# Graph layers on one core: VectorE reads a body's 18 tile numbers in one load, the sum banks go round in another order, and the mixer's rows are fetched between the two table stores

## The reference, cut to what matters

```python
for l in range(4):                                    # L0_gnn, one "loop" each below
    h = einsum('ni,rio->rno', X, W[l])                # the tables: one row per relation and node
    msg = h[etype, src] * inv_deg[:, None]
    agg = segment_sum(msg, dst)                       # 100,000 messages into 6,250 nodes
    out = agg + X @ root[l] + bias[l]
    X = elu(layer_norm(out) * gamma[l] + beta[l]) + X
...
qkv = x @ Wqkv.T                                      # L0_mix, on the same nodes
q, k = elu(q) + 1, elu(k) + 1
kv, ksum = k^T v, sum(k)                              # Keys0
x1 = layer_norm(q kv / (q ksum + eps) + x)            # Attend
y = layer_norm(gelu(x1 @ W1.T + b1) @ W2.T + b2 + x1) # Feed
...
agg = segment_sum(all_h[src, rel], dst)               # L1_gnn, 8 relations: loop gnn1
```

## Time and profile before

| | |
|---|---|
| median of 3 runs | 8250.26 us (8244.22 to 8263.54) |
| profiled execution, its own time | 8245.88 us |
| its span, first to last instruction | 8244.1 us |
| mean granted clock of TensorE | 0.823 |
| PE / PEld busy | 5874.8 us (71%) / 3559.1 us (43%) |
| DVE busy | 4269.0 us (52%) |
| ACT busy | 2931.9 us (36%) |
| POOL busy | 4208.5 us (51%) |

### The profile page before, as it was taken

The page is one execution under the profiler, slowest core; times in us unless marked ns, Lnnn a source line. Parts: engine busy times, 40 slices in busy tenths (PEclk is TensorE's granted clock), DMA queues, the critical chain, the costliest instruction groups (busy, mean ns, idle before and its releaser), DMA issues. The chain is left out here.

```text
span 8244.1 us, 110504 instructions
## 1 busy us (share of the span) xinstructions
PE 5874.8 (71%) x17886; PEld 3559.1 (43%) x17886; DVE 4269.0 (52%) x14582; ACT 2931.9 (36%) x8048; POOL 4208.5 (51%) x4288
## 2 busy tenths in 40 slices
PE   0487777767777776777768888788498777763398
PEld 0244444444444444554443333355344444443265
DVE  7215555546666665666656666522434666652412
ACT  0133333333444445666653333222022444431132
POOL 0016666656666656777667777600002777753211
PEclk9998888888888888889985556589599888877699
DMA  1444333334444434444443333300044333330000
GB/s 56 145 132 118 112 116 114 113 115 121 124 124 123 123 117 134 135 135 135 132 151 105 104 105 105 99 0 0 19 142 132 105 105 105 105 87 1 13 14 18
DMA packets 478956, 811.01 MB, mean 98 GB/s; under 512 B 88600, under 2 KB 343148, under 8 KB 478657
## 3 DMA queue, kind: packets, MB, share of 16 engines
q0 software_dynamic: 200480, 548.02, 23.2%
q1 hardware_dynamic: 278430, 262.51, 9.9%
HBM read 614.04 MB, written 196.16 MB: 98 GB/s over the span
## 5 line engine op out<-in xcount | busy, mean ns | idle before, releaser
L530 POOL DMA_INDIRECT gnn_msg<-tables,gnn_row_ring x4165 | 3985.8, 957 | 2183.9 <-issue 1585.2
L579 PE MATMUL bank<-gnn_msg,gnn_hot 128*128 128x256 f32 x8330 | 3143.3, 494 | 781.0 <-DVE sums L559 506.8
L559 DVE TENSOR_TENSOR sums<-sums,bank 128x256 f32 x4165 | 1746.0, 419 | 2060.0 <-PE bank L579 1360.7
L579 PEld LDWEIGHTS bank<-gnn_msg,gnn_hot 128*128 128x128 f32 x8330 | 1748.2, 237 | 2130.3 <-DVE sums L559 1424.8
L133 POOL TENSOR_TENSOR ve<-mv,eps 128x7 f32<-128x7 f32 x35 | 7.1, 204 | 1348.6 <-DVE mv L127 1200.3
L520 ACT ACTIVATE gnn_hot<-gnn_away,gnn_meta_ring 128x128 f32<-128x128 f32 x1568 | 645.8, 482 | 47.3 <-ACT gnn_meta_ring L511 0.8
L684 PE MATMUL bank<-gnn_w,residual 128*128 128x512 f32 x1176 | 620.1, 610 | 33.7 <-DVE sums L652 33.7
L508 ACT ACTIVATE gnn_away<-iota,gnn_meta_ring 128x128 f32<-128x128 f32 x1960 | 625.5, 391 | 24.0 <-ACT gnn_meta_ring L498 0.2
L539 DVE TENSOR_SCALAR gnn_hot<-iota,gnn_meta_ring 128x128 f32<-128x128 f32 x1764 | 629.1, 357 | 0.5 <-ACT gnn_meta_ring L498 0.5
L497 ACT COPY gnn_row_ring<-row 128x9 int32 (+1 forms) x490 | 94.9, 194 | 1070.3 <-PE bank L579 1058.5
L1760 PE MATMUL bank<-tables_w,sums 128*128 128x512 f32 x784 | 340.1, 596 | 6.4 <-ACTq L117 6.4
(11 more groups left out here) (390 smaller groups left out, 6866.1 us busy)
## 6 DMA issues: line engine op xcount, KB each, us to landing
tables<-residual SPq DMA_DIRECT2D x294, 256.0 KB
gnn_msg<-tables,gnn_row_ring POOLq DMA_INDIRECT x4165, 2.8
tables<-sums SPq DMA_DIRECT2D x98, 512.0 KB, 2.9
tables<-gnn_msg SPq DMA_DIRECT2D x98, 256.0 KB, 2.1
residual<-first_norm_columns SPq DMA_DIRECT2D x98, 128.0 KB, 2.4
first_norm<-state SPq DMA_DIRECT2D x1, 6272.0 KB, 21.4
first_rows<-residual SPq DMA_DIRECT2D x1, 6272.0 KB, 39.2
residual<-first_norm SPq DMA_DIRECT2D x49, 128.0 KB, 3.1
```

The costliest lines, as they stand in the source:

```text
L530: self.nc.gpsimd.indirect_dma_start(out=self.msg[:, s0 + u, :], out_offset=None, in_=table, in_offset=bass.IndirectOffsetOnAxis(ap=self.ro ...
L559: self.nc.vector.tensor_tensor(at, at, self.sums(s), ALU.add).then_inc(self.added, 1)
L579: self.nc.tensor.matmul(self.sums(s), self.hot[:, s, :], self.msg[:, s, :], start=True, stop=True).then_inc(self.summed, 1)
```

## The change

Four edits. (1) A row with 18 numbers for each body (the 17 tiles and the tile to finish) takes the place of the flat row, and VectorE loads all 18 at the body's start. (2) The banks of the 17 steps are a written list. (3) `sync` is split into `load` and `store`; the load for body i + 1 stands between the two table stores of body i. (4) Some hooks move to other steps: TensorE's mixer products, and in Attend two VectorE operations change places.

```diff
-SUM_SLOTS = 4
+SUM_BANKS = (4, 5, 6, 7, 4, 5, 6, 7, 4, 5, 6, 4, 5, 6, 4, 5, 6)
...
-def load_tiles(eng, c, first, n):
-
-    regs = c.regs[str(eng.engine)][:n]
-    eng.reg_load(regs, c.tile_row[0:1, ds(first, n)])
+def body_tiles(eng, c, i):
+
+    regs = c.regs[str(eng.engine)]
+    eng.reg_load(regs, c.body_row[0:1, ds(i * (SLOTS + 1), SLOTS + 1)])
     return [eng.snap(r, min_val=0, max_val=NT - 1) for r in regs]
...
-                sp.dma_start(c.tile_row[:], c.tl_d.rearrange("(a n) -> a n", a=1)).then_inc(s_tr, 16)
+                sp.dma_start(c.body_row[:].rearrange("p (i n) -> p i n", n=SLOTS + 1)[:, :, 0:SLOTS],
+                             c.tl_d[0:(NT + 1) * SLOTS].rearrange("(a i n) -> a i n", a=1, n=SLOTS)).then_inc(s_tr, 16)
...
+                ends_of = c.body_row[:].rearrange("p (i n) -> p i n", n=SLOTS + 1)[:, :, SLOTS]
+                then(v.tensor_copy(ends_of[:, 0:1], key[0:1, 0:1]))
+                then(v.tensor_copy(ends_of[:, 1:NT + 1], key[0:1, :]))
...
     def sums(self, s):
-        return self.c.bank[4 + s % SUM_SLOTS][:, 0:D]
+        return self.c.bank[SUM_BANKS[s]][:, 0:D]
...
-            tiles = load_tiles(dve, self.c, i * SLOTS + s0, w)
-            for u, t in enumerate(tiles):
+            for u in range(w):
                 s = s0 + u
+                t = tiles[s]
...
-            back = s - SUM_SLOTS + 1 if s >= SUM_SLOTS else max(k for k in range(SLOTS) if k % SUM_SLOTS == s) + 1 - SLOTS
-            pe.wait_ge(self.added, n * SLOTS + (SLOTS + back))
+            before = max(k for k in range(s - SLOTS, s) if SUM_BANKS[k] == SUM_BANKS[s])
+            pe.wait_ge(self.added, n * SLOTS + (SLOTS + before + 1))
...
 # Keys0.tensor and Attend.tensor
-            if s == 5 and first:
+            if s == 3 and first:
...
 # Attend.vector: L961 to step 6, L964 to step 9
-            if s == 9 and first:
+            if s == 6 and first:
                 dve.wait_ge(self.s_act, i * 2 + 3)
                 v.scalar_tensor_tensor(self.et, self.et, 1.0, self.rt, ALU.min, ALU.add).then_inc(self.s_q, 1)
-            if s == 6 and second:
+            if s == 9 and second:
                 dve.wait_ge(self.s_hat, i + 1)
                 v.tensor_tensor(self.u, self.u, self.vec[:, 0, :], ALU.mult).then_inc(self.s_gam, 1)
...
 # Feed.tensor: steps 3, 6, 10 become 2, 5, 9
...
-                    work.sync(sp, 0, True, False)
-                    with sp.Fori(1, NT) as i:
-                        work.sync(sp, i, True, True)
-                        post.sync(sp, i + l * NT, ranked_tile(sp, c, i - 1), c.tabs[(l + 1) % 2])
-                    work.sync(sp, NT, False, True)
-                    post.sync(sp, (l + 1) * NT, ranked_tile(sp, c, NT - 1), c.tabs[(l + 1) % 2])
+                    work.load(sp, 0)
+                    work.store(sp, 0, True, False)
+                    work.load(sp, 1)
+                    with sp.Fori(1, NT - 1) as i:
+                        t = ranked_tile(sp, c, i - 1)
+                        work.store(sp, i, True, True)
+                        post.sync(sp, i + l * NT, t, c.tabs[(l + 1) % 2], 0)
+                        work.load(sp, i + 1)
+                        post.sync(sp, i + l * NT, t, c.tabs[(l + 1) % 2], 1)
+                    for i in (NT - 1, NT):
+                        t = ranked_tile(sp, c, i - 1)
+                        work.store(sp, i, i < NT, True)
+                        for j in range(2):
+                            post.sync(sp, i + l * NT, t, c.tabs[(l + 1) % 2], j)
...
-                        t = ranked_tile(dve, c, i - 1)
-                        edges.vector(dve, i, n, both(post.vector(dve, n, t, work.cols), work.vector(dve, i, True, True)))
+                        tiles = body_tiles(dve, c, i)
+                        edges.vector(dve, tiles, n, both(post.vector(dve, n, tiles[SLOTS], work.cols),
+                                                         work.vector(dve, i, True, True)))
...
-        c.tile_row = sb("tile_row", [1, SB * P], I32)
+        c.body_row = sb("body_row", [1, (NT + 1) * (SLOTS + 1)], I32)
```

More of the change, by code:

```diff
@@ L548, in begin_vector, with vector @@
             self.one_hot(0, u)
-    def vector(self, dve, i, n, after, last=False):
+    def vector(self, dve, tiles, n, after, last=False):
         for h, (s0, w) in enumerate(HALVES):
-            tiles = load_tiles(dve, self.c, i * SLOTS + s0, w)
-            for u, t in enumerate(tiles):
+            for u in range(w):
                 s = s0 + u
+                t = tiles[s]
                 dve.wait_ge(self.summed, n * SLOTS + (SLOTS + s + 1))
@@ L701, in way_out, with sync @@
         self.nc.scalar.copy(self.outs[:, j, :], self.c.bank[3 - 2 * j][:]).then_inc(self.s_out, 1)
-    def sync(self, sp, n, t, table):
-        for j in range(2):
-            sp.wait_ge(self.s_out, n * 2 + (j + 1))
-            sp.dma_start(table.rearrange("(r n) d -> n r d", n=NP)[ds(t * P, P), 2 * j:2 * j + 2, :],
-                         self.outs[:, j, :].rearrange("p (r d) -> p r d", d=D)).then_inc(self.s_store[j], 16)
+    def sync(self, sp, n, t, table, j):
+        sp.wait_ge(self.s_out, n * 2 + (j + 1))
+        sp.dma_start(table.rearrange("(r n) d -> n r d", n=NP)[ds(t * P, P), 2 * j:2 * j + 2, :],
+                     self.outs[:, j, :].rearrange("p (r d) -> p r d", d=D)).then_inc(self.s_store[j], 16)
 def tile_columns(c, i):
@@ L731, in begin_sync, with load, store @@
         sp.dma_start(self.wt, self.c.wt_d[:, :, D:3 * D]).then_inc(self.s_in, 16)
-    def sync(self, sp, i, first, second):
-        if first:
-            sp.wait_ge(self.s_mm, i + 1)
-            sp.dma_start(self.xt.rearrange("p h r -> p (h r)"), tile_columns(self.c, i)).then_inc(self.s_xt, 16)
+    def load(self, sp, i):
+        sp.wait_ge(self.s_mm, i + 1)
+        sp.dma_start(self.xt.rearrange("p h r -> p (h r)"), tile_columns(self.c, i)).then_inc(self.s_xt, 16)
+    def store(self, sp, i, first, second):
+        return None
     def end_sync(self, sp):
@@ L896, in begin_sync, with load, store @@
         sp.sem_inc(self.s_dma, 16)
-    def sync(self, sp, i, first, second):
+    def load(self, sp, i):
         c = self.c
-        if first:
-            sp.wait_ge(self.s_u, i + 1)
-            sp.dma_start(self.xt.rearrange("p h r -> p (h r)"), tile_columns(c, i)).then_inc(self.s_xt, 16)
-            sp.dma_start(self.x, c.xn_d[ds(i * P, P), :]).then_inc(self.s_x, 16)
+        sp.wait_ge(self.s_u, i + 1)
+        sp.dma_start(self.xt.rearrange("p h r -> p (h r)"), tile_columns(c, i)).then_inc(self.s_xt, 16)
+        sp.dma_start(self.x, c.xn_d[ds(i * P, P), :]).then_inc(self.s_x, 16)
+    def store(self, sp, i, first, second):
+        c = self.c
         if second:
@@ L1008, in begin_sync, with load, store @@
         sp.sem_inc(self.s_put, 16)
-    def sync(self, sp, i, first, second):
+    def load(self, sp, i):
+        sp.wait_ge(self.s_u, i + 1)
+        sp.dma_start(self.x, self.c.rows_d[ds(i * P, P), :]).then_inc(self.s_dma, 16)
+    def store(self, sp, i, first, second):
         c = self.c
-        if first:
-            sp.wait_ge(self.s_u, i + 1)
-            sp.dma_start(self.x, c.rows_d[ds(i * P, P), :]).then_inc(self.s_dma, 16)
         if second:
@@ L1041, in after @@
         def after(s):
-            if s == 3 and first:
+            if s == 2 and first:
                 pe.wait_ge(self.s_dma, i * 16 + 16)
@@ L1046, in after @@
                 self.turn(pe, self.x, c.bank[0])
-            if s == 6 and first:
+            if s == 5 and first:
                 pe.wait_ge(self.s_xt, i + 1)
                 self.by_columns(self.w1)
-            if s == 10 and first:
+            if s == 9 and first:
                 pe.wait_ge(self.s_act, i * 2 + 3)
@@ L1371, in _ @@
                     gate(dve, c)
-                    edges.vector(dve, 0, l * NT, work.vector(dve, 0, True, False))
+                    edges.vector(dve, body_tiles(dve, c, 0), l * NT, work.vector(dve, 0, True, False))
                     dve.wait_ge(s_vec, l * 48 + 96)
@@ L1382, in _ @@
                 gate(dve, c)
-                edges.vector(dve, 0, LASTL * NT, nothing)
+                edges.vector(dve, body_tiles(dve, c, 0), LASTL * NT, nothing)
                 dve.wait_ge(s_vec, LASTL * 48 + 96)
@@ L1386, in _ @@
                     n = i + LASTL * NT
[L1387 to L1390 removed]
+                    tiles = body_tiles(dve, c, i)
+                    edges.vector(dve, tiles, n, post.vector(dve, n, tiles[SLOTS], 1, last=True))
+                tiles = body_tiles(dve, c, NT - 1)
+                edges.vector(dve, tiles, DEPTH * NT - 1, post.vector(dve, DEPTH * NT - 1, tiles[SLOTS], 1, last=True), last=True)
                 t = ranked_tile(dve, c, NT - 1)
@@ L2491, in program @@
                    (("pe", nc.tensor), ("act", nc.scalar), ("dve", nc.vector), ("pool", nc.gpsimd), ("sp", nc.sync))}
-        c.regs = {str(e.engine): [e.alloc_register(f"tile{u}") for u in range(HALF)] for e in (nc.vector,)}
```

(1 more changed line is left out.)

10 lines of the change are left out of this document (3 added, 7 removed).

## The result

The changed kernel takes 8053.94 us (median of 4 runs, 8048.98 to 8055.62), the kernel before 8256.88 us on the same chip (4 runs, 8244.22 to 8263.54): a ratio of 0.9753, 95% interval 0.9738 to 0.9767. The forecast was 8054.

A forecast was written before the change was run, and what follows sets the result against it. GpSimd's issue bounds loop 3 and gnn1, an alternating VectorE and TensorE chain loops 0 to 2. Terms of -33, -149, -10, 0 and 1 us of preparation, hidden or not, sum to -192 from 8245.9: 8054 us, range 7980 to 8185.

The forecast's parts named there:

- One load at the seam: Between bodies, add 16 to add 0: mean 4.5 us against 3.8 now, so 0.7 us longer.
- The load model: VectorE's register loads: 0.08 us fixed, 0.22 per number alone, 0.265 per four together; 18 numbers take 1.58 or 4.05 us.
- the first rival: The 18-number load is never short: seams of 6.08 us in loops 0 to 2, total 8284 us, slower; 9%.
- No load in the middle: Before add 9 in a body: the idle time of the second register load goes, 1.38 us on average.
- Banks at nothing: New bank order of the 17 steps: costs or gains nothing in loops 0 to 2; GpSimd hides waits elsewhere.
- The early fetch: Mixer rows fetched between the table stores, some 3.2 us earlier: gives 0.1 us a body at most in Feed.
- Mixer steps: TensorE's mixer products at earlier steps (5 to 3; Feed 3, 6, 10 to 2, 5, 9): fill seam idle.
- Loop 0, -33: Keys0's loop: -1.38 + 0.7 = -0.68 us a body over 48 bodies, -33 us.
- Attend's swap, L937 at 8.2, chain of 9.6: Loop 1: L937 starts 8.2 us after add 0, then 9.6 to add 16; body 22.3 against 25.4 us, -149 us.
- The third rival: GpSimd becomes the bound in loop 1: +0.4 us a body, 8075 us, inside the forecast's range; no chance given.
- The rule on register loads: Rule against the forecast: about 200 ns a register even for bulk, so 18 numbers take 3.6 us and gathering saves nothing.
- The fourth rival: More comes free: Feed's idle reaches the chain, TensorE's clock is granted more; 1 us a body in loops 0 and 2, 7960 us; 12%.

The follow-up runs named there:

- both experiments on the address: Changed kernel with rows of 20 numbers, every load starting at a multiple of 16 bytes, or none: 7932.8 us and 8287.3 us.
- the load alone: Kernel before with the single load of 18 numbers a body and nothing else of the change: 8138.9 us, ratio 0.9860.
- rows of 20: Changed kernel with 20 numbers per body in the row, 18 used, every load starting at a multiple of 16 bytes: 7932.8 us, ratio 0.9609.
- the fetch behind: Changed kernel with the mixer's next rows fetched behind the second table store again: 8024.7 us, ratio 0.9720 against the kernel before.

## Why the prediction was right, and where it wasn't

The total was right to the microsecond, which is luck: loops 0 and 1 gained 64 us more than forecast, loop 2 lost 50 us against its forecast, and the stretches between and the last two loops lost some 15 us that had no term.

1. *One load at the seam, mean +0.7.* Right: 4.45, 4.49 and 4.44 us in loops 0 to 2, against 3.84, 3.90 and 3.70 (+0.6 to +0.7). The load model read from four rows held for 18 numbers, 1.57 and 4.05 (in the loops with stores the long ones take a median of 4.6, where 4.72 was forecast), and both experiments on the address confirmed it, with the first rival's 8284 as 8287.
2. *No load in the middle, -1.38.* Right at its place (-1.43 to -1.54 between adds 8 and 9). Of it Feed passes on less than the 0.8 that I took: with the load alone, Feed's adds 9 to 16 took 7.22 us against 6.45, and adds 0 to 8 11.28 against 11.01, so only 0.39 of 1.43 reached the end, less than the seam's 0.77. That is the first wrong step: Feed loses 18 us from the load itself.
3. *Banks at nothing.* Right, within 8 us.
4. *The early fetch, 0.1 us at most in Feed.* Wrong in sign: it costs 21 us in loop 2 and 29 in the kernel, although the wait it was to remove (3.40 to 0.45 us) did go. What it sets off in loop 2 is open (below).
5. *Mixer steps "fill the idle at the seam", cost nothing.* Wrong, the dearest miss. They cost 42 us in loop 0 and 19 in loop 2. In the earlier trace rows I looked at who waits for whom, and not at how long the same matmul takes where it stands; L791's 275/422 was to be seen in the trace of before. That is the mistake for loop 0. The 19 us of loop 2 are not the clock's: with the steps back it is as it was (0.68 against 0.67 from add 0 to add 9, 1.00 in both from there to add 16), and what changes is the wait at L879.
6. *Loop 0, -33.* The two load terms as measured make -0.83 us a body (-40 us), and adds 9 to 16 got 0.27 shorter, which had no term. But that is what two large effects left: the load alone gives 105 us, 2.1 us a body and not 0.68, because without the middle load the second half came at the high level in 30 bodies of 42 instead of 3 (L795 median 276, L791 422) and took 9.09 us instead of 10.34; the rest of the change, almost all of it step 5 of this list, took 44 back.
7. *Attend's swap, L937 at 8.2, chain of 9.6.* The mechanism is right and the size too small. L944 starts at 8.76, and the chain behind it takes 8.67 in the body shown and 8.52 on average. The 9.6 was right for the kernel before (mean 9.67), where much of Post's product L678 ran at the low level:

```profile
L678 PE MATMUL bank<-gnn_w,residual x192: 379/634/635, 1879.5 to 3082.0; 128*128 128x256 f32 x192
```

```profile
L682 PE MATMUL bank<-gnn_w,residual x192: 379/379/483, 1815.9 to 2840.2; 128*128 128x256 f32 x192
```

   These are loop 1 before and after: a median of 634 ns, now 379; 135 of 192 records were at the low level, now none. It is the swap that does it: none are with the swap alone, 138 with it undone, and the granted clock from add 9 to add 16 is 0.77 before, 0.78 with the swap undone, 0.94 changed and 1.00 with the swap alone. TensorE without its gap of four microseconds is granted the high level for what follows. So the fall went on until GpSimd stopped it. The third rival (GpSimd becomes the bound in loop 1) came true, at a lower level than it was priced.
8. *The rule on register loads* (the Trainium skill, "Runtime: NRT & Kernel Launch", "Instruction fetch mechanics", 200 ns a register even for bulk): long loads agree, 4.04/18 = 0.22 us; short ones are 1.57/18 = 0.09, and rows of 20 make every load short. That page of the Trainium skill speaks of registers loaded from HBM; here the numbers lie in SBUF.

The fourth rival (TensorE waits less and is granted its clock more often) named the mechanism and gave it to the wrong loops at 12%: the granted clock between first and last add rose from 0.842 to 0.848 in loop 0 and from 0.847 to 0.866 in loop 1, and fell from 0.893 to 0.824 in loop 2; the mean of the kernel fell from 0.823 to 0.809.

**What stays open.** In loop 2 the two ways to undo the earlier work are each worth 20 us and together no more (1157.7 with neither, in the run with the load alone). The clock is not what they share: from add 9 to add 16 it is 1.00 in all of these kernels, and from add 0 to add 9 it is 0.82 in the kernel before, 0.67 in the changed one, and 0.68 to 0.71 with either or both undone; with Feed's steps back 339 of the 384 records of L879 are still at the low level, with the fetch behind 192. The wait for L1073 they do share: 177.6 us, against 112.6, 99.4 and 69.1. Why 65 to 109 us less of this wait bring 19 to 22 us each time isn't shown. Loop 0 with the fetch behind is as long as with it early (1172.9 against 1173.3), by a longer first half (9.20 against 8.65) and a shorter second one (9.51 against 10.07): delay and clock cancel there. Why short seams lower loop 0's clock (0.75) is open too.

## What to carry to other kernels

Before you cost a moved instruction at nothing, look whether it was what kept TensorE at work in a stretch: compare the minimum and the median of one matmul's duration. If they stand apart as 275 and 422 ns do here, work moved into an idle seam can slow what follows later in the body, and taking away a wait of four microseconds can also speed up the products behind it (634 to 379 ns in loop 1). Put the numbers that an engine loads into registers at once at multiples of 16 bytes, padding the rows if need be. And check a forecast by its stretches: a right total may be two wrong ones.

## What was not expected of the hardware

- 18 numbers load into VectorE's registers in 1.57 us when the first lies at a multiple of 16 bytes and in 4.04 us or more otherwise; in the loops that store tables the long ones take up to 4.92 us, the short ones up to 1.82.
- More work for TensorE made a loop shorter (loop 0 by 18 us with three more products a body), and data that came earlier made one longer (loop 2 by 21 us).
- The second half of a body of loop 0 takes 8.6 us when TensorE's granted clock is 1.00 in it, and 9.7 to 11.4 us otherwise; one product moved by two steps decides in how many bodies it is 1.00 (2 or 30 of 42).
- The same step costs differ by place: three doubled products a body cost 60 us in loop 2 and 43 us in gnn1, and nothing in loops 1 and 3.
